# The embedding's bias in a vision transformer kernel: from a seventh matmul and a ScalarE copy to an addition on VectorE

## The reference

```python
y = einsum('nsi,oi->nso', patches, W) + b          # 192 outputs for each of 64*196 tokens
h = layernorm(y) * ln_w + ln_b                     # mean and variance over the 192
# attention: qkv of layernorm(h), rounded and clipped to 3 bits, 12 heads; relu-like
# quantised scores instead of a softmax; projection; added to h
# experts: 8 of them, one chosen per token by a router; gelu; added to h
```

## Time and profile before

| | |
|---|---|
| runs | 1001.50, 1002.27, 1003.41 us; median 1002.27 us |
| profiled execution | 1000.83 us |
| its span (first to last instruction) | 999.0 us |
| granted TensorE clock, mean | 0.98 |
| GpSimd busy | 510.9 us (51%) |
| matmul instructions | 8170 |
| VectorE instructions | 2854 |
| ScalarE instructions | 1516 |
| bytes moved by DMA | 52.48 MB, 53 GB/s |

### The profile page before, as it was taken

The page is one execution under the profiler, slowest core; times in us unless marked ns, Lnnn a source line. Parts: engine busy times, 40 slices in busy tenths (PEclk is TensorE's granted clock), DMA queues, the critical chain, the costliest instruction groups (busy, mean ns, idle before and its releaser), DMA issues.

```text
span 999.0 us, 24830 instructions
## 1 busy us (share of the span) xinstructions
PE 912.5 (91%) x8170; PEld 792.7 (79%) x8170; DVE 743.6 (74%) x2854; ACT 697.0 (70%) x1516; POOL 510.9 (51%) x890
## 2 busy tenths in 40 slices
PE   5677999999999999998889899999999999999887
PEld 4565888888888888887778788888888888887766
DVE  3677778788877878777776777878877877878663
ACT  1367777786887777776566777777777777778652
POOL 4534563736556463736626456363645656363432
PEclk9798899999999999999999999999999999999989
DMA  8221121211112121212101111121212111000000
GB/s 232 98 61 36 35 74 38 68 45 57 45 54 68 37 76 37 70 41 67 45 29 60 46 53 61 45 61 45 62 43 69 50 53 45 13 14 13 14 13 28
DMA packets 31332, 52.48 MB, mean 53 GB/s; under 512 B 4653, under 2 KB 17886, under 8 KB 31206
## 3 DMA queue, kind: packets, MB, share of 16 engines
q1 hardware_dynamic: 31206, 50.90, 16.7%
HBM read 41.25 MB, written 9.63 MB: 51 GB/s over the span
## 4 chain that ended last, share of the span: by engine, by line
PE 34%; DVE 7%; ACT 6%; issue 4%; POOL 1%; DVEq 0%; ACTq 0%; POOLq 0%
PE mixed_ps L778 7%; PE near_ps L637 6%; PE mixed_ps L768 6%; PE mixed_ps L628 5%; PE near_ps L719 3%; PE scores_ps L699 2%; ACT relu L888 2%; PE turn_ps L650 1%; ACT hid L923 1%; DVE k_b L1172 1%; DVE h L1212 1%; PE turn_ps L651 1%; DVE prob L1150 1%; PE mixed_ps L732 1%; PE mixed_ps L776 1%
## 5 line engine op out<-in xcount | busy, mean ns | idle before, releaser
L888 ACT ACTIVATE relu<-scores_ps,c_prob 98x784 uint16<-98x784 f32 x384 | 348.2, 907 | 138.0 <-PE scores_ps L699 113.5
L637 PE MATMUL near_ps<-we,x_sb 128*128 128x192 f32 x1176 | 259.4, 342 | 11.4 <-DMA const_sb<-in_const 7.4
L969 POOL TENSOR_TENSOR ve<-mv,const_sb 128x1 f32<-128x1 f32 x294 | 60.1, 204 | 365.5 <-DVE mv L1309 361.9
L637 PEld LDWEIGHTS near_ps<-we,x_sb 128*128 128x128 f32 x1176 | 196.3, 197 | 18.0 <-DMA const_sb<-in_const 7.4
L982 POOL TENSOR_TENSOR expd<-econst,below 128x8 f32<-128x8 f32 x98 | 161.7, 1664 | 49.2 <-DVE below L1239 49.2
L972 POOL TENSOR_TENSOR rs<-ve,const_sb 128x1 f32<-128x1 f32 x294 | 174.4, 593 | 23.1
L1150 DVE TENSOR_SCALAR prob<-relu 98x784 bf16<-98x784 uint16 x384 | 151.2, 394 | 9.9 <-ACT relu L888 1.4
L778 PE MATMUL mixed_ps<-w_sb,hid 128*128 128x192 f32 x784 | 145.9, 330 | 0.0
L778 PEld LDWEIGHTS mixed_ps<-w_sb,hid 128*128 128x128 f32 x784 | 125.6, 191 | 1.3
L923 ACT ACTIVATE hid<-mixed_ps,b_sb 128x384 f32<-128x384 f32 (+1 forms) x128 | 72.9, 584 | 38.5 <-PE mixed_ps L768 38.3
L1125 DVE TENSOR_SCALAR xn<-h,mv,rs 128x192 f32<-128x192 f32 x196 | 74.2, 378 | 33.8 <-POOL rs L972 33.5
(11 more groups left out here) (154 smaller groups left out, 2212.9 us busy)
## 6 DMA issues: line engine op xcount, KB each, us to landing
x_sb<-in_x SPq DMA_DIRECT2D x98, 384.0 KB, 3.0
out<-out_sb SPq DMA_DIRECT2D x98, 96.0 KB, 1.6
we<-in_tok_w SPq DMA_DIRECT2D x1, 576.0 KB, 4.1
w_sb<-in_w SPq DMA_DIRECT2D x1, 384.0 KB
hid<-in_w_qkv SPq DMA_DIRECT2D x1, 288.0 KB
hid<-in_w_qkv SPq DMA_DIRECT2D x2, 144.0 KB
hid<-in_w SPq DMA_DIRECT2D x1, 256.0 KB
hid<-in_w SPq DMA_DIRECT2D x2, 128.0 KB
```

The costliest lines, as they stand in the source:

```text
L637: pe.matmul(dst, x_sb[:, tile % X_RING, j], we[:, j], start=j == 0, stop=False)
L888: act.activation(relu16[:, u % 2], scores_ps[0:KEYS, 2 * (u % VISIT):2 * (u % VISIT) + 2, 0:2 * SEQ], ACT.Relu, scale=c_prob[0:KEYS, :]).t ...
```

## The change

The seventh matmul goes, and with it the half of the constants and of the split that made its operands. The bias is loaded as it is, in f32, broadcast over 128 partitions (`tokb`). `embed_evac` moves from ScalarE to VectorE and becomes an addition of `near_ps` and `tokb` into `y1`. It stands no longer at the end of slot s of ScalarE, but at the very head of slot s+1 of VectorE, ahead of `low_experts`. Its semaphore is now `dve_y`, which `stats1` and the next users of `near_ps` wait for. ScalarE's later step `norm1` needs no wait for it, since it waits for `bias1`, as before. The tables of slots stay as they are. The number of VectorE's setup steps falls by one.

```diff
-C_FIRST = C_PART + 3
-C_HALFNEG, C_E, C_EPS = (C_FIRST + TT + n for n in range(3))
+C_HALFNEG, C_E, C_EPS = (C_PART + 3 + n for n in range(3))
...
-        c[8 * j, C_FIRST:C_FIRST + TT] = 1
...
-        raw_24 = sb("raw_24", [24, 2 * EMBED], f32)
+        raw_24 = sb("raw_24", [24, EMBED], f32)
+        tokb = sb("tokb", [TT, EMBED], f32)
...
-        rows24 = sb("rows24", [128, 2, EMBED], bf16)
-        parts24 = sb("parts24", [24, 3, 2 * EMBED], bf16)
-        first24 = sb("first24", [128, TT], bf16)
+        rows24 = sb("rows24", [128, EMBED], bf16)
+        parts24 = sb("parts24", [24, 3, EMBED], bf16)
...
-                            NEAR.append((i, s + 0.35, ("embed", tile), act_y, tile + 1))
+                            NEAR.append((i, s + 0.35, ("embed", tile), dve_y, tile + 1))
...
-        bias_loads += [(raw_24[8 * j:8 * j + 8, 0:EMBED], b2) for j in range(3)]
-        bias_loads += [(raw_24[:, EMBED:2 * EMBED], tok_b.partition_broadcast(24))]
+        bias_loads += [(raw_24[8 * j:8 * j + 8, :], b2) for j in range(3)]
+        bias_loads += [(tokb[:, :], tok_b.partition_broadcast(TT))]
...
-                pe.matmul(dst, x_sb[:, tile % X_RING, j], we[:, j], start=j == 0, stop=False)
+                last = pe.matmul(dst, x_sb[:, tile % X_RING, j], we[:, j], start=j == 0, stop=j == KC - 1)
                 if j == KC - 1:
-                    if tile == 0:
-
-                        pe.wait_ge(set_dve, SET_EMBED)
-                    pe.matmul(dst, first24[:, :], rows24[:, 1], start=False, stop=True).then_inc(embedded, 1)
+                    last.then_inc(embedded, 1)
...
-                pe.matmul(dst, one_t[:, cols], rows24[:, 0], start=True, stop=False)
+                pe.matmul(dst, one_t[:, cols], rows24[:, :], start=True, stop=False)
...
-            def embed_evac(tile):
-                act.wait_ge(embedded, tile + 1)
-
-                wait(act, act_n1, tile + 1 - Y_RING)
-                act.activation(y1[:, tile % Y_RING], near_ps[0:TT, 0:EMBED], ACT.Copy).then_inc(act_y, 1)
-
...
-                    for tile in first_at(EVAC1, one, s):
-                        embed_evac(tile)
...
-                split_b(bias_parts, raw_24[:, :], scratch_a[0:24, :])
+                split_b(bias_parts, raw_24[:, :], scratch_a[0:24, 0:EMBED])
...
-                setup(dve.tensor_copy(first24[:, :], const_sb[:, C_FIRST:C_FIRST + TT]))
...
+            def embed_evac(tile):
+                dve.wait_ge(embedded, tile + 1)
+
+                wait(dve, act_n1, tile + 1 - Y_RING)
+                dve.tensor_tensor(y1[:, tile % Y_RING], near_ps[0:TT, 0:EMBED], tokb[:, :], ALU.add).then_inc(dve_y, 1)
+
             def stats1(tile):
-                dve.wait_ge(act_y, tile + 1)
+                dve.wait_ge(dve_y, tile + 1)
...
                 for s in range(SLOTS + 1):
                     inside = s < SLOTS
+                    for tile in first_at(EVAC1, one, s - 1) if s else []:
+                        embed_evac(tile)
                     for g, tile in second_at(TURN3, two, three, s - 1) if s else []:
                         low_experts(g, tile)
```

More of the change, by code:

```diff
@@ L415, in vit_tower_kernel @@
         embedded = sem("embedded")
-        act_y = sem("act_y")
+        dve_y = sem("dve_y")
         dve_st1 = sem("dve_st1")
@@ L553, in vit_tower_kernel @@
         all_loads = [bias_loads, embed_loads, attention_loads, expert_loads, affine_loads]
-        SET_EMBED, SET_ATTENTION, SET_ALL = 10, 23, 48
+        SET_EMBED, SET_ATTENTION, SET_ALL = 9, 22, 47
         ROUTER_PRODUCT, PREPARE_PROJECTION, PREPARE_EXPERTS = 8, 4, 9
@@ L1033, in set_embedding @@
             def set_embedding():
-                setup(dve.memset(rows24[:, :, :], 0.0))
+                setup(dve.memset(rows24[:, :], 0.0))
                 come(dve, 0)
                 bias_parts = [parts24[:, j] for j in range(3)]
-                split_b(bias_parts, raw_24[:, :], scratch_a[0:24, :])
-                setup(dve.tensor_scalar(scratch_b[0:24, :], bias_parts[0], const_sb[0:24, C_PART:C_PART + 1],
+                split_b(bias_parts, raw_24[:, :], scratch_a[0:24, 0:EMBED])
+                setup(dve.tensor_scalar(scratch_b[0:24, 0:EMBED], bias_parts[0], const_sb[0:24, C_PART:C_PART + 1],
                                         None, ALU.mult))
                 for j in (1, 2):
-                    dst = scratch_b[0:24, :] if j == 1 else rows24[0:24].rearrange("p a b -> p (a b)")
+                    dst = scratch_b[0:24, 0:EMBED] if j == 1 else rows24[0:24, :]
                     setup(dve.scalar_tensor_tensor(dst, bias_parts[j],
                                                    const_sb[0:24, C_PART + j:C_PART + j + 1],
-                                                   scratch_b[0:24, :], ALU.mult, ALU.add))
-                setup(dve.tensor_copy(first24[:, :], const_sb[:, C_FIRST:C_FIRST + TT]))
+                                                   scratch_b[0:24, 0:EMBED], ALU.mult, ALU.add))
             def set_attention():
```

## The result

| | before | after |
|---|---|---|
| median of the runs, us | 1001.88 (4 runs) | 1014.25 (4 runs, 1011.21 to 1015.84) |
| profiled execution, us (span) | 1000.83 (999.0) | 1011.21 (1009.4) |
| after to before | | 1.0138, 95% interval 1.0112 to 1.0164 |

The account below looks back on a forecast made before the run. TensorE is nearly full, but VectorE releases set its starts at a few places. Steady passes 8.2 + 0.8 + 0.5 + 1 + 0.5 = 11.0 us on 1000.83 give 1011.8, as a median 1013; range 999 to 1019, the forecast's own 1008 to 1018.

Parts of the forecast that it names:

- TensorE, what goes: 98 bf16 matmuls leave TensorE, each worth 0.1 us, not under 0.08 nor over 0.25; 9.8 us in all without waits.
- Head of slot 2: First tile's addition on VectorE: av gains 0.05 us, statistics' delay of about 0.5 swallowed but for 0.05; nearly nothing won.
- Head of slot 5: Addition ahead of spread_evac starts the up projection 0.36 to 0.4 us later; pass at +0.38 at slot 6.
- Slots 8 and 11: Additions fit in VectorE's idle time there; TensorE keeps 0.08 and 0.1 us, leaving the pass at +0.2.
- Slot 14: Addition behind a 0.75 us quantise on VectorE makes TensorE's av start 0.14 us later; pass at about +0.35.
- Slot 17: Addition ahead of VectorE's gapless chain to the norm moves TensorE's turn by 0.3 us; pass at +0.68.
- First pass: Tile 3's addition must precede set_attention, moving the first turn 0.6 us; with tiles 5 and 6, +0.8.
- Other passes: Second pass +0.5 us, pass 8 +1 (between 0 and 3), pass 9 +0.5, last two 0.
- Loads: At the kernel's head, tok_b grows to 96 KB and const shrinks to 73: -0.2 to +0.5 us, taken as 0.
- TensorE alone decides: Rival: VectorE's releases have over 0.4 us of slack, so 9.8 us go and 992.5 results; chance 0.16.
- It cancels: Rival: slack or slot 5's relu leaves a steady pass within 0.1 us of before, 1000 to 1005; chance 0.12.
- Blocking spreads: Rival: VectorE blocking costs passes 8 and 9 4 us or more, steady passes some 0.9; 1018; chance 0.14.

Follow-up runs that it names:

- e8: Kernel after, but the first tile of each group of six keeps the seventh matmul and the ScalarE copy; 1011.68 us, ratio 1.0102.
- e3: Kernel after, but the second tile of each group of six keeps the seventh matmul and the ScalarE copy; 1012.85 us, ratio 1.0134.
- e5: Kernel before, but the third and fourth tile of each group of six are added on VectorE without the seventh matmul; 1000.51 us, ratio 1.0000.
- e9: Kernel after, but the fifth tile of each group of six keeps the seventh matmul and the ScalarE copy; 1014.38 us, ratio 1.0141.
- e4: Kernel after, but the sixth tile of each group of six keeps the seventh matmul and the ScalarE copy; 1012.87 us, ratio 1.0129.
- e10: Kernel after run and traced once more, unchanged; ratio 1.0120 to the kernel before.
- e0: Kernel before run and traced once more, unchanged; 1002.02 us in one run.
- e6: Kernel after, but all tiles of the two groups of seven keep the seventh matmul and the ScalarE copy; 1011.58 us, ratio 1.0112.
- e1: Kernel before with the seventh matmul alone taken out, leaving out the bias; ScalarE still copies; 997.65 us, ratio 0.9969.
- e11: Kernel before with only third and fourth tiles on VectorE, the tok_b broadcast moved to the end of the attention's loads; 997.87 us, ratio 0.9985.

## Why the prediction was right, and where not

The forecast was 1013, measured 1014.25; the steady pass 56.90, where 56.9 to 57.0 was said, with TensorE busy for 54.39 (about 54), up waiting 0.79 (about 0.9) and av in slot 14 waiting 0.22 (about 0.3). The mechanism held: additions in front of VectorE's releases reach TensorE. All parts of the steady pass but one stand in the trace where the working had put them; that the total comes so near is partly luck, as terms that were too large (8.2 for 7.4, and 1.0 for passes 1 and 9) stand against one that was missing (the load's 1.35). Step by step:

- **TensorE, what goes.** "I take 0.1", 0.08 for the sum's being ready. Locally right (0.08 or 0.09 at four places, 0.10 and 0.16 at the others), but as a gain of the pass it is 0.22 to 0.23 for six, 0.04 each, under the lower bound that I gave. That bound took for granted that nobody further on waits for anyone else.
- **Head of slot 2.** This step failed. I followed VectorE's own queue, saw the delay swallowed at the clip of the heads, and stopped. By the trace the delay had left through the aggregate to POOL and came back in nb, with the choice behind it. Measured 0.16 to 0.19 (e8) for "nothing lost, nearly nothing won".
- **Head of slot 5.** Said +0.38 at slot 6, with up waiting 0.9; measured +0.41 at slot 7 and 0.79. The figure holds by luck: with the first tile back on ScalarE it is +0.26 there (e8), and the place by itself costs 0.27 (e3). I had put 0.1 too much here, and the step left out in slot 2 made it good.
- **Slots 8 and 11.** Said 0.18 won; e5 won 0.17.
- **Slot 14.** Said 0.14, to stand at +0.35; measured 0.11, at +0.34 (slot 15); by itself 0.10 to 0.16 (e9).
- **Slot 17.** Said 0.33 more; the trace goes from +0.35 in slot 16 to +0.62 in slot 20, and e4 gives 0.28 to 0.30.
- **Steady passes.** Said 12 x 0.68 = 8.2; measured 7.4 in one pair of traces and 7.3 in the other (e10 less e0).
- **First pass.** Said +0.8, of which 0.6 up to the first turn. From the first matmul to the first turn it is 18.91 and 18.85 us (after, e10) against 18.31 (e0), so 0.5 to 0.6. From the first matmul to the start of pass 1 it is 42.65 and 42.54 against 41.20 (e0), and 41.88 in the first trace of before if the 1.75 us of its slow second tile are taken off: 0.7 to 1.4.
- **Other passes.** Pass 8, "+1, between 0 and 3": 0.2 to 0.9 at like clocks. Pass 9, "+0.5": -0.13 and -0.21. Pass 1, "+0.5": -0.78 in one pair and +0.23 in the other, with clocks of 0.88 and 0.84 before against 0.90 after. I had copied both from a steady pass; in pass 9 that cost isn't there, and in pass 1 the clock hides it if it is.
- **Loads.** "-0.2 to +0.5, I take 0": the means of the three first matmuls on each side are 7.92 and 9.27, so +1.35. I argued that const still comes last and is half as large. It is still what the first matmul waits for, but the 96 KB instead of 18 ahead of it count for more than its own smaller size. This term, put at 0, is the one most mis-sized.
- **Bounds.** Taken all at once they would give 1006.8 to 1021.8; 1008 to 1018 was a choice inside them.

The medians differ by 12.4 us, and by 11.6 in e10's group. Of this 7.4 are steady passes, 1.35 the load, 0.7 to 1.4 the first pass behind it, 0.2 to 0.9 pass 8. The remaining 0.5 to 3 us are not settled: how often the clock falls differs from execution to execution, and executions of programs that are alike up to pass 1 (e5, e6) differ there by 3.3 us, 1.9 of them in the matmuls of the second tile (2.19 and 4.09 us).

The rival "TensorE alone decides" is refuted by e1: without any addition a pass gains 0.22, not 0.6. The Trainium skill (Perfetto Trace Analysis, section Identifying the Most-Contended Engine) would have one work on the engine of the highest occupancy, and has TensorE's headroom judged by its weight loads and not by its matmul time. In the steady pass the weight loads take 47.88 of 56.27 us, 85%, and VectorE is busy for 79%, so TensorE is first by that measure too; followed by that alone, the advice misleads here. The Trainium skill (same page, section Optimizing Scalar/DVE Operations) makes VectorE's overhead on PSUM some 75 ns more than ScalarE's. Measured are whole durations, 356 ns for the addition against 325 for the copy, 31 more; the overheads by themselves no run here shows. "It cancels" needed a steady pass within 0.1 of the old one. "Blocking spreads" needed 4 us in pass 8, which the first pair of traces seems to show at 3.1 and e0 takes away.

## What to carry to other kernels

Work moved to an engine with 20% of its time free is charged at its place in the queue: the same trade, 356 ns more for VectorE and a matmul less for TensorE, cost 0.28 to 0.30 us at one place of a pass and won 0.17 at two others together. Follow what stands behind it, and follow each result that leaves the engine until it comes back; a delay that the engine's own next wait swallows may already be on its way through another engine. And before a pass's growth is put down to a change, take a second trace of the kernel before: here 2.9 us of 70 came and went with the granted clock.

## What the runs showed of the hardware

- In pass 8 the granted clock of TensorE fell below full in 13 of the 14 traces (means of 0.93 to 0.98) and stayed at 1.00 in the first one of the kernel before. In the kernel after it fell behind a stretch with TensorE busy for 1.62 of 5 us, in e0 behind one with 0.44 of 3; in the first trace of the kernel before the clock stayed at 1.00 through 0.44 of 3.
- POOL's reciprocal root (rs, 128x1) took 0.57 us in slot 2 before and 0.98 after, the same instruction at another moment beside VectorE. Over all 294 it ranges from 0.54 to 1.10 us in both kernels. Why was not tried.
- With a broadcast of 96 KB instead of 18 issued ahead of const, the first matmul, which waits for const, started 1.35 us later (means of three traces each, 7.92 and 9.27), though const had shrunk from 137 to 73 KB. With the broadcast moved behind, it started at 7.21 (e11).
